# The experts' bias rows as a six-row product in the weights' single-pass type, in place of a three-row product of 16 bits

## The reference

```python
x = x + 0.5 * _L0_ffn_ref(_layernorm(x), ...)   # first kind: 8 experts, one product, capacity 512
x = x + _L0_attn_ref(_layernorm(x), ...)
x = x + 0.5 * _L0_ffn_ref(_layernorm(x), ...)
x = x + 0.5 * _L1_ffn_ref(_layernorm(x), ...)   # second kind
x = x + _L1_attn_ref(_layernorm(x), ...)        # mixer
x = x + 0.5 * _L1_ffn_ref(_layernorm(x), ...)   # second kind, same weights
```

```python
def _L1_ffn_ref(x, Wg, bg, W1, b1, W2, b2):
    ...
    idx = jnp.argmax(gates, axis=-1)
    h = jax.nn.gelu(jnp.einsum('th,ehi->tei', xf, W1) + b1, approximate=False)
    y = jnp.einsum('tei,eih->teh', h, W2) + b2
    out = jnp.take_along_axis(y, idx[:, None, None], axis=1)[:, 0, :]
```

## Time and profile before

| | us |
|---|---|
| median of 3 runs | 1552.46 |
| lowest and highest of them | 1542.86, 1554.94 |
| the profiled execution, its own time | 1545.96 |
| span of the profiled execution, first to last instruction | 1544.7 |

### The profile page before, as it was taken

How to read it: one execution, slowest core, us unless ns; L and a number is a source line. 1 busy time by engine, 2 the same in 40 slices (tenths; PEclk the granted TensorE clock), 3 DMA queues, 4 the chain that set the end, 5 groups by cost and what they waited for, 6 DMA issues and landing times. The chain is left out here.

```text
span 1544.7 us, 30156 instructions
## 1 busy us (share of the span) xinstructions
PE 1147.4 (74%) x12088; PEld 898.3 (58%) x12088; DVE 973.6 (63%) x1669; ACT 813.9 (53%) x907; POOL 606.7 (39%) x610
## 2 busy tenths in 40 slices
PE   4464789199999989649999967463669928973998
PEld 2253666188888886448888853352258814631786
DVE  4213745799999954689999984137424447743454
ACT  4311453499999804279999956134323324471332
POOL 2753000825545410435454445560723311335233
PEclk9888799699999999869999989696779968975898
DMA  9578101312122000101221221463333240013232
GB/s 293 217 220 251 44 1 34 135 57 85 56 84 82 31 8 1 58 28 57 84 80 61 84 79 70 149 219 116 114 90 101 90 147 0 1 41 129 66 101 79
DMA packets 84588, 140.55 MB, mean 91 GB/s; under 512 B 10574, under 2 KB 71246, under 8 KB 79956
## 3 DMA queue, kind: packets, MB, share of 16 engines
q1 hardware_dynamic: 71396, 102.76, 20.7%
q0 software_dynamic: 13056, 35.87, 6.5%
HBM read 86.60 MB, written 56.24 MB: 92 GB/s over the span
## 5 line engine op out<-in xcount | busy, mean ns | idle before, releaser
L1167 ACT ACTIVATE b_signs<-b_q_everywhere,normed 128x2048 bf16<-128x2048 f32 x224 | 432.7, 1993 | 32.0 <-PE bank L1077 27.2
L1077 PE MATMUL bank<-b_value_parts,b_signs 128*128 128x102 bf16 x8192 | 408.0, 209 | 36.5 <-DVE b_signs L1308 26.7
L1077 PEld LDWEIGHTS bank<-b_value_parts,b_signs 128*128 128x128 bf16 x8192 | 378.3, 97 | 73.3 <-DVE b_signs L1308 70.6
L1308 DVE TENSOR_SCALAR b_signs<-b_q_everywhere,normed 128x2048 bf16<-128x2048 f32 x288 | 390.7, 1392 | 1.9 <-PE bank L1077 1.9
L543 POOL DMA_INDIRECT moe_slots<-normed,slot_of_token x128 | 124.8, 975 | 39.3 <-issue 33.5
L1369 POOL TENSOR_TENSOR normed<-b_sums,normed 128x16 f32<-128x16 f32 x32 | 34.8, 1087 | 249.4 <-DVE b_sums L1319 249.4
L359 PE MATMUL bank<-identity,normed 128*128 128x128 f32 x256 | 51.6, 338 | 63.2 <-ACT normed L335 46.9
L1345 POOL TENSOR_TENSOR b_signs<-b_signs,normed 128x1024 f32<-128x1024 f32 x8 | 22.0, 2756 | 160.8 <-DVE normed L1258 160.3
L308 DVE BATCH_NORM_STATS2 ln_stats<-residual 128x6 f32<-128x256 f32 x192 | 73.8, 419 | 17.8 <-DMA bg<-in_bg 7.7
L1069 PE MATMUL bank<-normed,ones_bf 128*128 128x408 bf16 x128 | 28.9, 350 | 69.5 <-DVE normed L1276 69.5
L368 PE MATMUL bank<-normed_T,wg 128*8 128x256 f32 x256 | 75.9, 425 | 0.0
(11 more groups left out here) (246 smaller groups left out, 2431.4 us busy)
## 6 DMA issues: line engine op xcount, KB each, us to landing
b_q_everywhere<-q_rows SPq DMA_DIRECT2D x32, 1024.0 KB, 4.7
normed<-expert_rows SPq DMA_DIRECT2D x9, 1024.0 KB, 10.3
d_rows<-moe_slots SPq DMA_DIRECT2D x40, 129.5 KB, 2.1
f_rows<-moe_slots SPq DMA_DIRECT2D x40, 129.5 KB, 2.1
moe_slots<-a_empty SPq DMA_DIRECT2D x8, 518.0 KB, 8.4
a_rows<-moe_slots SPq DMA_DIRECT2D x16, 259.0 KB, 3.6
moe_empty_slots<-a_empty SPq DMA_DIRECT2D x8, 518.0 KB, 5.3
moe_slots<-moe_empty_slots SPq DMA_DIRECT2D x1, 4144.0 KB
```

The costliest lines, as they stand in the source:

```text
L1077: ins = nc.tensor.matmul(banks[qt // QPB][:, qt % QPB * VP:(qt % QPB + 1) * VP], t.SG[:, (hh * TB + kt) % RING, qt * P:(qt + 1) * P], t.VO ...
L1167: nc.scalar.activation(t.SG[:, g % RING, :], t.QB[:, hh % 2, :], ACT.Sign, bias=t.NKT[:, kt, hh % H:hh % H + 1]).then_inc(s.sign_a, 1)
L1308: nc.vector.tensor_scalar(t.SG[:, g % RING, :], t.QB[:, hh % 2, :], t.KTM[:, kt, hh % H:hh % H + 1], 2.0, ALU.is_gt, ALU.mult).then_inc(s. ...
```

## The change

The bias product takes the weights' type. Its stationary operand is now `LAYER`, six rows by 128 columns in float32r for each layer: ones in rows 0 to 2 and zeros in rows 3 to 5 for the first layer, and the reverse for the second. Its moving operand is one table of six rows, `B_PARTS`, that holds the three parts of both layers' biases in float32r. The parts are split and stored in 4 bytes in place of 2. They are read back into `B_RAW`, and ACT copies them in place into `B_PARTS` (the same bytes, under the other type) at the end of the third stage; PE waits for that copy where it waited for the read. POOL makes `LAYER` at the program's start. The statistics `z_stats` of the attention stage move into a free piece of `normed`, which makes room.

```diff
-    k.bias_parts = nc.dram_tensor("bias_parts", [2, 3, E * D], BF16, kind="Internal").ap()
+    k.bias_parts = nc.dram_tensor("bias_parts", [2, 3, E * D], F32, kind="Internal").ap()
...
-    k.BIAS3 = m.take("top1_bias_parts", [P, 2, 3, E * D // P], BF16)
+    k.BIAS3 = m.take("top1_bias_parts", [P, 2, 3, E * D // P], F32R)
+    k.LAYER, k.LAYERF = m.take("rows_of_layer", [6, 2, P], F32R), m.take("rows_of_layer_f", [6, 2, P])
...
-    k.B_PARTS = [w.take(f"b{n + 1}_parts", [3, E * D], BF16) for n in range(2)]
+    k.B_RAW = Area(nc, "", w.at).take("bias_parts_raw", [6, E * D])
+    k.B_PARTS = w.take("bias_parts_in", [6, E * D], F32R)
...
-                nc.sync.dma_start(k.B_PARTS[layer][:, :], k.bias_parts[layer]).then_inc(s.bparts_in, 16)
+                nc.sync.dma_start(k.B_RAW[3 * layer:3 * layer + 3, :], k.bias_parts[layer]).then_inc(s.bparts_in, 16)
...
+        if r == 1 and n == pairs - 1:
+            nc.scalar.wait_ge(s.bparts_in, 32)
+            nc.scalar.activation(k.B_PARTS[:, :], k.B_RAW[:, :], ACT.Copy).then_inc(s.bparts, 1)
...
-    nc.tensor.wait_ge(s.bparts_in, 32)
+    nc.tensor.wait_ge(s.bparts, 1)
...
-        last = nc.tensor.matmul(out, k.ONESB[0:3, :], k.B_PARTS[layer][:, where], start=False, stop=True)
+        last = nc.tensor.matmul(out, k.LAYER[:, layer, :], k.B_PARTS[:, where], start=False, stop=True)
...
+    nc.gpsimd.memset(k.LAYERF[:, :, :], 1.0)
...
+    for layer, (base, step) in enumerate(((2, -1), (-3, 1))):
+        ins = nc.gpsimd.affine_select(out=k.LAYERF[:, layer, :], in_=k.LAYERF[:, layer, :], compare_op=ALU.is_ge, fill=0.0, base=base,
+                                      pattern=[[0, P]], channel_multiplier=step)
+    k.ps.step(ins)
+    nc.gpsimd.tensor_copy(k.LAYER[:, :, :], k.LAYERF[:, :, :])
```

More of the change, by code:

```diff
@@ L109 @@
     "back0 back1 back2 y0_zeroed empty_stored spares_stored y_in0 y_in1 y_in2 y_in3 y_in4 "
-    "raw_in bparts_in split_hi split_lo "
+    "raw_in bparts_in bparts split_hi split_lo "
     "m_turned m_hi m_lo m_first m_hs m_hturned m_hhi m_hlo m_second m_ys "
@@ L234, in plan_attention @@
     t.HELD3 = xn[:, at:at + H * VP // 2].bitcast(BF16).rearrange("p (h c) -> p h c", h=H)
-    assert at + H * VP // 2 <= NT * RW
+    at += H * VP // 2
+    t.ZST = xn[0:H, at:at + 48].rearrange("p (q c x) -> p q c x", q=2, c=4)
+    assert at + 48 <= NT * RW
     t.W1R = m.take("hidden_weights", [P, 2, KD, D], F32R)
@@ L260, in plan_attention @@
     t.MB = m.take("means_everywhere", [P, KD, P])
-    t.ZST = m.take("z_stats", [H, 2, 4, 6])
     t.ZMV = m.take("z_mean_var", [H, 2, 2])
@@ L560, in sp_moe0 @@
             nc.sync.wait_ge(s.bias_split, n + 1)
-            nc.sync.dma_start(k.bias_parts[n].rearrange("i (p c) -> p i c", p=P), k.BIAS3[:, n, :, :]).then_inc(s.bias_stored, 16)
+            nc.sync.dma_start(k.bias_parts[n].rearrange("i (p c) -> p i c", p=P), k.BIAS3[:, n, :, :].bitcast(F32)).then_inc(s.bias_stored, 16)
     nc.sync.wait_ge(s.scattered, 16 * NT * (r + 1))
@@ L700, in pool_moe0 @@
                 k.ps.step(ins)
-                k.ps.step(nc.gpsimd.tensor_tensor(k.BIAS[:, n, :], k.BIAS[:, n, :], k.BIAS3[:, n, i, :], ALU.subtract))
+                k.ps.step(nc.gpsimd.tensor_tensor(k.BIAS[:, n, :], k.BIAS[:, n, :], k.BIAS3[:, n, i, :].bitcast(F32), ALU.subtract))
         nc.gpsimd.wait_ge(s.y0_zeroed, 16)
```

## The result

The changed kernel takes 1571.3 us (median of 4 runs, 1568.33 to 1574.52), the kernel before 1552.28 us. The ratio is 1.0134, with a 95% interval of 1.0092 to 1.0177: slower by 19 us. The profiled execution took 1574.06 us, with a span of 1572.7.

What follows compares the result with a forecast made beforehand. TensorE's serial sequence, busy throughout the two changed stages, was taken as the bound. 151 x 0.11 = 16.6 us plus 9 x 0.20 = 1.8 us gave 18.4 us; added to 1550.8, 1569 us, range 1554 to 1580.

Steps and rivals of the forecast that it cites:

- The array empties by shape, so both gaps stay: Around the bias product on TensorE: shape, not type, empties the array, so both 0.21 us intervals stay; forecast held at 70%.
- The rival in which the entry's gap falls: Ahead of the bias product: type empties the array there, so that gap goes; 14.4 us less, about 1536; 10%.
- the one in which both fall: Around the bias product: nothing empties, all products take 0.12 us; 42 us less, about 1509; 3%.
- 0.11 us for each product at full clock, 0.20 at half: From the bias's load to the next: 0.32 us in place of 0.21; at half clock 0.17 + 0.35 - 0.32 more.
- Some nine products: Bias products at half clock: the first one and eight in the last stage up to 1440 us; together 1.8 us.
- forecast 18.4: All 160 bias products in TensorE's sequence: 16.6 us at full clock plus 1.8 us at half, added to the time.
- Six rows load like 128: Bias's float32r load: a bare load takes 0.11 us whatever the rows, its record about 0.18 us in place of 0.09.
- The cheaper load of that rival: Bias's float32r load takes 0.06 us in place of 0.11; 9 us in all, about 1559; 10%.
- The side work is free: ACT's 1.90 us copy after its third-stage work and POOL's about 1 us at the start stay hidden under waits.
- The clock: Rival: more emptiness lets the granted clock fall back inside a stage, losing some 8 us more; 1577; 7%.
- a level between median and mean: Base for the sum: 1550.8 us, between the earlier runs' median 1552.46 and mean 1549.05, giving 1569.

Runs made afterwards that it cites:

- experiments 1: Kernel before, its 16-bit bias product widened from 3 to 128 rows with zeros: 1507.62 us beside 1549.42, ratio 0.9707.
- second experiment: Changed kernel, its float32r bias product widened from 6 to 128 rows with zeros: 1505.61 us, ratio 0.9721 to the kernel before.
- 6: Kernel before, with the second tile's bias product moved to its tile's start, right behind the first tile's: 1529.13 us beside 1547.27, ratio 0.9865.
- the two profiles: Profiled executions of the changed kernel: one from its first measurement (1574.06 us), one from its later runs on another chip.
- the repeat: Changed kernel run again, unaltered, beside the kernel before on another chip: 1588.77 us beside 1572.85, ratio 1.0103.
- experiment 3: Whole change but the type (six rows, selecting operand, side work, all in 16 bits) against the kernel before: 1549.13 us, ratio 1.000.
- 8: Kernel before, its 16-bit bias product widened to 65 rows with zeros: 1508.91 us in one run, beside 1547.27.

## Why the prediction was right

*The array empties by shape, so both gaps stay.* Right, and shown: the gaps are in the changed kernel as they were, they vanish with equal shape in either type (experiments 1, 2) and halve in number with half the visits (6). The rival in which the entry's gap falls, and the one in which both fall, are refuted for six rows.

*0.11 us for each product at full clock, 0.20 at half.* Measured 0.10 (0.31 in place of 0.21) and 0.19 (0.51 in place of 0.32). Some nine products were forecast at half the clock; the two profiles have 17 and 12. The sums are 17.5 and 17.1 us (143 x 0.10 + 17 x 0.19 and 148 x 0.10 + 12 x 0.19); forecast 18.4. Measured by medians: 19.0 us, and 1.03% or 16 us in the repeat. That the 19.0 lies nearer to 18.4 than to 17 is luck: the forecast was 0.01 us too high for each product, and the rest of the 19.0 is the clock or the spread of the runs.

*Six rows load like 128.* Right within 0.01 us: the record is 0.18 us against 0.19 for 128 rows. The cheaper load of that rival (0.06) is not seen.

*The side work is free.* Right: experiment 3 bounds all of it, with the parts in 2 bytes, at 0.0% with an interval of 0.2% to each side. ACT's copy took 1.89 us in idle time, forecast 1.90; POOL's start came 1.2 us later (4.51 in place of 3.31 us), forecast 1.

*The clock.* I gave 7% to a clock that falls back inside a stage, and it doesn't. What it does in both profiles is rise later, which I had not thought of. The first of the two stages of the profiled execution is 17.5 us longer, of which some 9 are the bias products and the rest goes with the clock; it is a part of the 28 us by which that execution is longer than the profile of before. A forecast against single profiled executions would have been off by these 10 us. The choice to add the sum to a level between median and mean, 1550.8, came out at 1569 against 1571.3; the kernel before had 1552.28 in the end, and from there the sum gives 1570.7.

## What to carry to other kernels

A small product between full ones costs its visit: the array empties on the way in and on the way out, and the loads there lie bare. Here that was 42 to 44 us for 160 visits, 0.26 to 0.27 us each. Widen the small product with zero rows until it takes the same part of the array (65 rows were enough here, 64 were not), or put the small ones side by side; its type matters only where its load is bare, and there 16 bits are the cheaper. The version to take is the first or second experiment. There TensorE begins to wait for the ring of row buffers, so that is where to look next.

## What the runs showed of the hardware

- A load of 128 columns with nothing to hide it holds up the next load by 0.01 to 0.02 us in 16 bits (3 rows in experiment 6, 128 in the earlier trace rows), and in float32r by 0.10 to 0.11 at the full clock and 0.17 at half, for 6, 64 or 128 rows. The Trainium skill ("TensorE: Matmul & The Clock Gate", section "Weight-path perf modes — Fast Weight Load (FWL) and DoubleRow") gives the fast mode about a factor of two. The lengths of the records here agree with that (0.09 us in 16 bits, 0.18 in float32r, for few rows); the time until the next load was nearer to a tenth, and it is this time that the kernel pays.
- From float32r to 16 bits in one shape the load is not pulled ahead: it begins with its product's slot, 0.12 us behind the product before it (experiments 1 and 8), where a float32r load begins beside it. The slot of the product is 0.12 us in both, so it costs nothing here.
- A TensorE that the trace shows as busy did not get the full clock in every kernel. With two six-row float32r products for each tile the granted clock stayed at 1.2 GHz through both stages, 218 us each (95.00 of 95.00 us busy in one stretch), and the kernel took 1754.88 us, 184 more than with one such product. With 64 rows in the same sequence, or with two three-row 16-bit products, it rose to 2.4 GHz, on another chip.
